# Asking for a layer norm's next tiles at the head of SyncE's step, in a fused two-layer cross-attention kernel

## What is computed

```python
# block 0
ln_out = layernorm(hidden_states, ln1_s, ln1_b)
q, k, v = split(ln_out @ w_qkv + b_qkv)
x = hidden_states + merge_heads(attention(q, k, v, ltor_mask)) @ w_ao + b_ao      # phase A
ln_out = layernorm(x, ln2_s, ln2_b)
q = ln_out @ w_q + b_q;  k, v = split(encoder_states @ w_kv + b_kv)
x = x + merge_heads(attention(q, k, v, cross_mask)) @ w_co + b_co                 # phase B
ln_out = layernorm(x, ln3_s, ln3_b)
x = x + gelu(ln_out @ w1 + b1) @ w2 + b2                                          # the MLP
# block 1
a = layer_norm(audio_kv, ln_gamma, ln_beta)
Q, K, V = x @ Wq.T, a @ Wk.T, a @ Wv.T
x = x + tanh(gate) * (attention(Q, K, V) @ Wo.T)                                  # phase D
```

## Time and profile before

| | |
|---|---|
| time, median of 3 runs | 1095.85 us (1093.7 to 1096.87) |
| the profiled execution: its own time | 1097.2 us |
| its span, first to last instruction | 1095.6 us |
| PE (TensorE matmul) busy | 1066.8 us, 97% |
| DVE busy | 820.2 us, 75% |
| ACT busy | 704.0 us, 64% |
| POOL busy | 482.2 us, 44% |
| 16 DMA engines | mean 170 GB/s, 185.92 MB moved |

### The profile page before, as it was taken

One profiled execution on the slowest core, in us unless ns is written; L12 is line 12 of the kernel. 1 busy time (PEld: TensorE's weight loads), 2 busy tenths in 40 slices (PEclk: granted clock), 3 DMA queues, 4 the chain that ended last, 5 costly groups with the idle time before them and its releaser, 6 DMA issues.

```text
span 1095.6 us, 24221 instructions
## 1 busy us (share of the span) xinstructions
PE 1066.8 (97%) x8741; PEld 925.3 (84%) x8741; DVE 820.2 (75%) x1299; ACT 704.0 (64%) x2354; POOL 482.2 (44%) x361
## 2 busy tenths in 40 slices
PE   7999999999999999999999999999999999999998
PEld 6888888888888888887898888888888988888886
DVE  6688787777887788888867667767697466666767
ACT  4687777777888778887444444434455276666676
POOL 3665665657667676777613113113032232222210
PEclk9999999999999999999999999999999999999999
DMA  6356666576777777564243251341647636666621
GB/s 217 105 188 204 201 188 190 175 221 206 215 223 220 210 229 235 162 192 162 68 146 103 79 173 58 116 133 60 212 134 258 224 123 207 208 203 210 204 66 60
DMA packets 145831, 185.92 MB, mean 170 GB/s; under 512 B 17856, under 2 KB 88752, under 8 KB 145712
## 3 DMA queue, kind: packets, MB, share of 16 engines
q1 hardware_dynamic: 145712, 184.37, 53.7%
HBM read 122.59 MB, written 61.73 MB: 168 GB/s over the span
## 4 chain that ended last, share of the span: by engine, by line
PE 53%; DVE 16%; ACT 9%; POOL 6%; DMA 6%; issue 5%; SPq 3%; DVEq 0%; ACTq 0%
PE psum L1089 15%; PE psum L1070 14%; PE psum L892 11%; POOL prob L2207 6%; PE psum L884 4%; PE psum L1009 4%; ACT prob L1374 4%; DVE ln_tile L1689 3%; ACT prob_blocks L1374 2%; DVE negmax L1767 2%; DVE prob L1754 2%; DMA normalised<-ln_tile 2%; PE psum L910 2%; ACT inputs_transposed L1412 1%; DMA ln_tile<-stream 1%
## 5 line engine op out<-in xcount | busy, mean ns | idle before, releaser
L892 PE MATMUL psum<-inputs_hi,weights_hi 128*128 128x256 f32 x768 | 223.9, 292 | 3.6 <-DVE v L1815 1.7
L892 PE MATMUL psum<-inputs_lo,weights_hi 128*128 128x256 f32 x768 | 217.1, 283 | 0.0
L892 PE MATMUL psum<-inputs_hi,weights_lo 128*128 128x256 f32 x768 | 216.9, 282 | 0.0
L2207 POOL TENSOR_TENSOR prob<-prob,mask_bias 128x1024 f32<-128x1024 f32 x64 | 152.9, 2410 | 101.4 <-DVE prob L1754 99.3
L892 PEld LDWEIGHTS psum<-inputs_hi,weights_hi 128*128 128x128 f32 x768 | 146.6, 191 | 9.2 <-DVE v L1815 1.9
L1767 DVE TENSOR_REDUCE negmax<-prob 128x8 f32<-128x1024 f32 x96 | 115.6, 1211 | 48.1 <-POOL prob L2207 48.0
L1374 ACT ACTIVATE prob<-prob,negmax 128x128 f32<-128x128 f32 x384 | 148.3, 392 | 0.1
L892 PEld LDWEIGHTS psum<-inputs_lo,weights_hi 128*128 128x128 f32 x768 | 147.0, 191 | 0.2
L892 PEld LDWEIGHTS psum<-inputs_hi,weights_lo 128*128 128x128 f32 x768 | 146.9, 191 | 0.0
L2193 POOL TENSOR_TENSOR inputs_lo<-inputs_transposed,inputs_hi 128x512 fp32r<-128x512 f32 x70 | 93.3, 1353 | 91.6 <-DVE inputs_hi L1727 59.3
L1374 ACT ACTIVATE prob_blocks<-prob,negmax 128x128 f32<-128x128 f32 x304 | 117.5, 390 | 24.1 <-DVE negmax L1767 23.9
(11 more groups left out here) (132 smaller groups left out, 2655.4 us busy)
## 6 DMA issues: line engine op xcount, KB each, us to landing
prob_turned<-prob_blocks SPq DMA_DIRECT2D x38, 512.0 KB, 3.0
prob<-prob_turned SPq DMA_DIRECT2D x152, 128.0 KB, 3.4
weights_whole<-weights_in SPq DMA_DIRECT2D x72, 256.0 KB, 3.4
inputs_transposed<-normalised SPq DMA_DIRECT2D x120, 128.0 KB, 2.9
normalised<-ln_tile SPq DMA_DIRECT2D x24, 512.0 KB, 2.8
context<-row_sums_spread SPq DMA_DIRECT2D x188, 64.0 KB, 2.1
stream<-residual SPq DMA_DIRECT2D x42, 256.0 KB, 2.7
ln_tile<-stream SPq DMA_DIRECT2D x32, 256.0 KB, 3.9
```

The lines of the kernel that those rows point to most:

```text
L892: mm = pe.matmul(ps[:, bank, GT * part:GT * part + GT], w[:, slot, c, o], a[:, buf, c, :], start=c == 0 and i == 0, stop=c == KC - 1 and i ...
L2207: pool.tensor_tensor(half, half, mb.unsqueeze(1).to_broadcast([128, 8, T]), ALU.add).then_inc(s_biased, 1)
```

## The change

The call that loads the tiles of the next but one normalised input moves within SyncE's step, from behind `load_stream` to the step's head. Its condition is the same, so it happens in the same steps: g = 2, 4, 6, 8 in phase A, and 12, 14, 16, 18, 20, 22, 24, 26 and 29 (12 and 14 belong to A, the others to B). In the other steps where tiles are loaded (behind `store_normalised`) nothing moves.

```diff
                 ahead_ln = st.ahead and st.ahead.ln is not None and st.ahead.kind == HERE
                 if g in (44, 45, 46):
                     load_mask(D, st.b + 1)
+                if st.later and st.later.ln is not None and not ahead_ln and g:
+                    load_tiles(st.later)
                 if st.ends and g not in (2, 34):
                     store_stream(g - 3)
                 if g - 1 in WHOLE:
...
                 if st.ends and st.phase != D:
                     load_stream(g - 2)
-                if st.later and st.later.ln is not None and not ahead_ln and g:
-                    load_tiles(st.later)
                 if g - 1 in WHOLE:
                     bring_second_blocks(g - 1)
```

## The result

| | before | changed |
|---|---|---|
| median of 7 runs each, us | 1094.95 (1093.7 to 1097.04) | 1102.05 (1099.68 to 1104.91) |
| ratio, 95% interval | | 1.0062, 1.0044 to 1.0081 |
| profiled span, us | 1095.6 | 1098.0 |

The changed kernel is about 0.6% slower, 7 us, and lies 0.55 us above the top of the predicted range. Its runs spread over 5.2 us, those of before over 3.3. The profiled execution is its fastest: 1099.68 us, with a span of 1098.0.

What follows compares the result with a forecast made beforehand. PE, busy 97% of the span, was taken as the bound, with 4.0 us of waits to win. The terms summed to +0.6 us on 1095.85, giving 1096.5 us; 8 in 10 range 1093.0 to 1101.5.

Steps and rivals of the forecast that it cites:

- the tile waits: DVE's seven waits for stream tiles at a layer norm's statistics, 4.7 us together; all were counted as gone.
- waits before L986: PE's waits before its product with the turned blocks, expected new: 0.4, 1.5 and 1.25 us in steps 18, 20, 22.
- the spread row sums: Sign to look for: DVE waits for them in L1796 in most steps after 14.
- step 18: Phase B: blocks 0.4 us late after 1.1 us of slack, with no idle PE time to absorb it; +0.4 us.
- the five steps together: Steps 12, 14, 16, 24, 26, bounded by steps 8 and 18 (2.0 us in all) and taken as +0.3 us.
- d: Delay in landing of the transfers behind the moved pair; between 0.9 and 1.9 us, taken as 1.5.
- Steps 20 and 22: Phase B: late blocks set against PE's waits for the row sums; +0.3 us and -0.4 us.
- The two long waits before L949: PE's waits for inverse row sums around 340 and 370 us, 1.16 and 1.62 us; expected to go to nothing.
- Steps 2 to 8: Phase A: 1.5 us of delay out of 2.5 us of slack, covered by PE's projection work; nothing.
- The residual tile: Late by d; GpSimd's 2.06 us before the next mask addition covers 1.5, and 1.9 only just; no cost.
- Rival 2: The row sums' round trip becomes phase B's bound: +7.7 us, 1103.5; chance of over 3.3 us by this 0.2.
- The base: Median of the kernel before, 1095.85 us, to which the sum was added; the profiled execution's own time was 1097.2.

Runs made afterwards that it cites:

- only_b: The changed kernel with the pair of tile loads moved to the head only from step 12 on; 1101.71 us, ratio 1.0055 to the kernel before.
- behind_sums: The changed kernel with the pair placed behind the turned blocks and the row sums' store, ahead of the residual tile only; 1100.80 us, ratio 1.0045.
- behind_blocks: The changed kernel with the pair placed behind the stream's store and the turned blocks, ahead of the row sums' store; 1099.28 us, ratio 1.0033.
- late30_old: The kernel before, with GpSimd waiting for DVE's context parts of item 30 before adding that item's bias row; 1095.25 us, ratio 0.9996.
- again: The changed kernel run once more without edit, for a second profiled execution and more times; 1101.17 us, ratio 1.0048 to the kernel before.
- order_head: The changed kernel, with GpSimd adding the bias row to the residual tile behind its subtractions; 1102.71 us, ratio 1.0084 to the kernel before.
- order_old: The kernel before, with GpSimd adding the bias row to the residual tile behind its subtractions; 1099.53 us, ratio 1.0034.
- head_store_last: The changed kernel with the stream's store moved behind blocks, row sums and residual tile in the moved steps; 1097.08 us, ratio 1.0039.

## Why the prediction was wrong

The direction of the sum was right and its mechanisms mostly were: the tile waits went, waits before L986 and for the spread row sums came. The size was not: +0.6 us predicted, 6 to 7 measured. Two terms of the sum failed, step 18 and the five steps together: +0.7 us predicted, +3.0 and +4.4 in the two executions. Both rest on the same thing, that d stays under 1.9 us and that every step begins on time. Below, what a step did is read from the pair of products around it, against the first trace of before.

- **d itself.** I took 1.5 us, between 0.9 and 1.9. From the first issue behind the turned inputs to the last block's landing, step 22 took 366.7 - 360.59 = 6.1 us before and 369.4 - 361.80 = 7.6 now: 1.5. But it varies: by 1.0 in step 20, and in step 18, counted from PE's product before, by about 2.1, more than the 1.9 that I had for its most. In step 22 it is 0.95 us of later issue, 0.1 of slower issuing and 0.4 of longer landing. My bound took it that transfers land in the order of issue. Nearly all do: of 971 transfers of the trace before, 19 landed ahead of the one issued just before them.
- **Step 18: +0.4. This term failed.** Its pair of products took 1.5 us more in one execution and 3.3 in the other. PE waited 1.02 and 1.86 us before L986, since d was near 2 there, and 0.4 before L949 in the first; in the second the clock fell as well.
- **Steps 20 and 22: +0.3 and -0.4.** Measured -0.6 and +0.1 over the pairs of steps in the first execution, -1.4 and +1.6 in the second. The two long waits before L949 went as predicted, and waits of 0.34 and 1.45 us before L986 came (predicted 1.5 and 1.25).
- **Steps 12, 14, 16, 24, 26: "+0.3 us together". This term failed too.** Measured +1.5 and +1.1. Steps 14 and 24 gave 0.9 and 1.1 us in the first execution, step 16 took 0.5 off. I had bounded them by two other steps and had not read them. In step 24 the blocks had 2.2 us of slack, more than d. It was still used up, because the lateness carries over on SyncE: in step 23 the wait of L680 for the row sums ends 2.0 us later, behind it stands the store of the normalised tiles, and behind that the turned inputs, the last thing that SyncE issues ahead of step 24. SyncE's queue before, then the changed kernel's:
```profile
384.86 0.38 SPq L529 DMA_DIRECT2D normalised<-ln_tile  x1
386.01 0.33 SPq L621 DMA_DIRECT2D prob_turned<-prob_blocks  x1
388.12 1.82 SPq L555 DMA_DIRECT2D inputs_transposed<-normalised  x4
389.99 0.45 SPq L655 DMA_DIRECT2D stream<-residual  x1
390.48 1.88 SPq L630 DMA_DIRECT2D prob<-prob_turned  x4
```
```profile
386.38 0.38 SPq L529 DMA_DIRECT2D normalised<-ln_tile  x1
387.07 0.33 SPq L621 DMA_DIRECT2D prob_turned<-prob_blocks  x1
390.67 1.81 SPq L555 DMA_DIRECT2D inputs_transposed<-normalised  x4
392.53 0.92 SPq L520 DMA_DIRECT2D ln_tile<-stream  x2
393.49 0.43 SPq L655 DMA_DIRECT2D stream<-residual  x1
393.97 2.00 SPq L630 DMA_DIRECT2D prob<-prob_turned  x4
```
  The turned inputs are issued 2.55 us later, PE's last product (item 22) only 1.15. The other 1.4 us come on top of the pair's own delay: 0.4 of them stand already at the store of the normalised tiles, and 1.0 is its longer way from issue to landing (4.2 us, before 3.2), for which the turned inputs wait. SyncE's waits before L680 between 95 and 455 us rose from 51.6 to 62.9 us. I had let every step begin on time.
- **Steps 2 to 8: nothing.** Nearly so: 0.3 us in step 4, and `only_b` finds no share of theirs. But phase A's pace did change, which I had named as a sign of being wrong: step 14 belongs to it.
- **The residual tile: "1.5 is covered; at 1.9 only just", costed at nothing.** The cover that I read the earlier trace rows was the one before GpSimd's mask addition. What matters is the work between: in step 20 L2168 ends 0.36 us ahead of DVE's two-input product, and 1.84 us later it falls on it. This costs 0.45% where it stands alone (`behind_sums`), and less in the changed kernel (excess +1.3 and +2.5 us in its two executions, waits for v 0.3 and 1.4).
- **Rival 2, the row sums' round trip, +7.7.** Its number was nearest and its mechanism is half true: DVE waits 7.2 us for the spread, but PE's waits before L949 fell, where the rival needed them to grow. Only in `behind_blocks`, with the blocks on time, do they stand at 4.3. What the late row sums cost by themselves stays open; no run had them alone late.
- **The base.** I set the sum against a profile whose own time is 1097.2 us and which has two long waits before L949. The 97 executions of the kernel before beside these runs have a mean of 1095.3. The second trace, `late30_old`, has 2.4 us of waits before L949 in place of 4.0: there was less stock to win than the first trace showed, while I counted the gain from that trace in full. And a slow execution of before was set against the fastest of seven of the changed kernel, and their spans, +2.4, show under half of the median's +7.
- **Not in the sum at all.** Step 31, 2.6 us in `again` and about 1 at the end, and the falls of the clock, perhaps 0.5 us net.

How the loss splits is not shown. Late blocks and late row sums together cost 0.3 to 0.5% without any collision (`order_head` against `order_old`). The waits before L986 alone account for a fifth to a half of the loss: without them 0.33% stay in `behind_blocks` and 0.39% in `head_store_last`, of 0.48 to 0.62%. Step 31 is perhaps 1 us, the clock less. What late row sums cost alone stays open, and the parts replace one another: each run that takes one away leaves or brings another.

## What to carry to other kernels

A load that is early by a whole step gains what PE waited for, here 2.8 us at most, and delays by its bytes all that stands behind it in the same queue; read the slack of each of those transfers in every step, not in two, and follow where the queue's own waits pass lateness on to its next step. If a transfer must go ahead, move something that nobody waits for (here a store) behind in exchange. When a transfer releases GpSimd, look which DVE operation with two SBUF inputs its later work will fall on.

## What the hardware showed that I had not expected

- A GpSimd subtraction that shifted by 1.9 us lengthened a pair of DVE products from 0.76 to 2.33 us, though neither waits for the other in the program; another such collision, on L1856, made it 1.78 us for 0.69.
- Two idle stretches of PE of 1.86 and 1.98 us in an otherwise full engine were each followed by 1.2 GHz for most of three microseconds, with 32 products in 2.07 and 2.09 us in place of 1.17. The steps behind them took 0.9 and 1.0 us more than in the execution without falls, about half of the wait on top of it.
